# Mean-free output weight and centroids with closed norms in an attention and expert kernel

## The chip, the cores and the metric

One program on one core of a Trainium2 chip. The metric is the device time of one execution in microseconds (us), taken over several executions. The span of a profiled execution is the part of it that the hardware profiler covers. Names of engines: PE is TensorE (PEld its weight loads), DVE is VectorE, ACT is ScalarE, POOL is GpSimd, SP is SyncE, which here only issues DMAs.

## The reference, cut to what matters

The input is 16 batches of 256 tokens of width 128. Attention has 16 heads of width 8 and is causal; behind it come 8 experts with 512 hidden units each, of which each token uses one.

```python
x  = L0_attn_x                                     # 16 x 256 x 128, float32
y  = attention(layernorm(x))                       # V and output weight WO at its end
x2 = x + layernorm(y)
f  = layernorm(x2)
aff    = f @ centroids.T                           # 8 affinities for each token
assign = argmax(aff);  alpha = sigmoid(max(aff))
h  = layernorm(f, ln_g[e], ln_b[e])                # the inner norm, e = assign
z  = alpha * (relu(h @ w1[e].T + b1[e]) @ w2[e].T + b2[e])
out = x2 + layernorm(f + z)
```

## The kernel before

**Stages.** (1) A start: loads, constants, norms of x, and the first projections. (2) The attention loop. (3) A hand-over in which the counts of tokens for each expert become routing tables. (4) The expert stage over 39 tiles of 128 tokens that are sorted by expert. Each engine has a hand-written order; the engines are tied to each other by counted semaphores alone.

**The attention loop** is 20 iterations over 16 batches, software-pipelined. Iteration i works on batch i+3 (`new`: transposes of x and the projections to Q and K), i+1 (`nxt`: scores by query, to find their maxima), i (`t`: scores by key, exponentials, weighing of V), i-1 (`old`: transposes of the output, division), i-2 (`l2`: output projection, norm of y, x2, norm of x2), i-3 (`l3`, `ln`: affinities, choice of the expert) and i-4 (`l4`, `last`: rank within the expert, and the rows to DRAM). PE's iteration has four groups of heads (0 to 3).

- Q and K are split in three bf16 parts: ACT takes the high part from PSUM, DVE forms the residue, ACT the middle part, and POOL the low part (`low`, line 407). SP writes the parts to DRAM (`parts_out`, line 283) and reads them back in the layout of `aug` by six DMAs (`parts_in`, lines 294 and 296). The negated maxima go to `aug` by a DMA too (`shift`, line 306). `scores_near` (line 826) of group 0 waits for that last one.
- `project_qk` (line 773), the transposes and all small products of PE share one PSUM bank, M. Whoever takes it waits until the one before has been copied out (`take_m`).
- The norms of y and x2: DVE takes statistics (line 1115), aggregates (1122) and adds epsilon (`ln_variance`, 1128), POOL raises to the power -1/2 (`power`, 424), DVE applies (`ln_apply`, 1133). This is done three times for each batch: n=0 for y, n=1 for x2, which gives f, and n=2 for f, which is the inner norm. `add_y` (1144) forms x2. PE transposes f (`transpose_f`, 882) and multiplies it with the centroids (894).
- POOL's iteration is: four `select` (the causal mask, lines 413 and 417), with `power` 0 and 1 of batch i-2 between them, then `scatter(last, 0)` (an indirect DMA of 128 rows, line 439), `power(ln, 2)`, `scatter(last, 1)`, `number` (429) and at the end `low` of batch i+3.
- A row in DRAM (`xs_rows`) has 262 floats: f, x2 and six columns.

**The expert stage** is a second software pipeline. At step t: SP loads the weights w1 of a later tile (line 350, a ring of four buffers) and its rows (359, a ring of 14); ACT normalises rows of tile t+3 (702) and, after PE's transpose (976), applies the expert's gain and bias (`enter`, t+2, 721); PE multiplies with w1 (`up`, t+1, 986), ACT and DVE each take two of four relus (731 and 1374), and PE multiplies with w2 (`down_`, t, 999). DVE then handles tile t-1: `add_bias` (1381), `residual` (1389), `statistics` (1394), `aggregate` (1398), `variance` (1403). POOL forms the deviation's inverse (`power_z`, 515) and the bias (`bias_z`, 521), ACT applies both (`apply`, 711), DVE adds x2 (`add_x`, t-3, 1411) and POOL writes the rows of tile t-3 out by an indirect DMA (`leave`, 505). The number of the expert of a tile is only known on the chip: `expert` loads it to a register (`value_load`, which appears as TENSOR_LOAD) on SP, ACT, PE and DVE, since columns and weights are addressed by it.

## Time and profile before

| | us |
|---|---|
| three runs | 473.40, 473.89, 471.58 |
| their median | 473.4 |
| the profiled execution | 472.17 |
| its span | 470.4 |
| outside the span | 1.77 |

| engine | busy us of the span | share |
|---|---|---|
| PE | 364.0 | 77% |
| PEld | 288.5 | 61% |
| DVE | 356.6 | 76% |
| ACT | 255.5 | 54% |
| POOL | 259.7 | 55% |

The mean granted clock of TensorE is 0.928 of full speed. No engine is busy all the time, and the shares are means over stages with different limits. The stages by time: the attention loop in its steady state from about 50 to 290 us, its last iterations to 342, the hand-over to about 363, and the expert stage from there to the end. A row of a timeline has the start, the duration, the engine, line, operation, output<-input, a count if like rows follow each other, and in brackets how long the engine had been idle before it and what released it.

### The profile page before, as it was taken

The page shows a single profiled execution, that of the slowest core. Times are in us where ns is not written, and L with a number is a line of the kernel's source. Part 1 is how long each engine was busy: PE and PEld are TensorE (multiplying, and loading weights), DVE is VectorE, ACT ScalarE, POOL GpSimd, SP SyncE. Part 2 cuts the span into 40 slices and gives each one's busy share as a digit, 9 for nine tenths or more (in the row PEclk, how much of TensorE's full clock was granted, in tenths as well). Part 3 has the DMA queues.
Part 4 walks back from the last instruction along what each step waited for, and adds up shares of the span by engine and source line. Part 5 has one row for each costly group of instructions (what it writes and reads, how often), then busy time and mean ns, then how long its engine had stood idle before and what let it go on. Part 6 is the DMA issues. An engine that isn't in the chain of part 4 may idle for free.

```text
span 470.4 us, 12290 instructions
## 1 busy us (share of the span) xinstructions
PE 364.0 (77%) x3737; PEld 288.5 (61%) x3737; DVE 356.6 (76%) x1281; ACT 255.5 (54%) x574; POOL 259.7 (55%) x388
## 2 busy tenths in 40 slices
PE   3268798798997998798898988986308988888850
PEld 2146566576675776676676766854307877878740
DVE  7658588789989988888878897977532777777770
ACT  2205466566665666567566554672105777776740
POOL 4804425535466467456455565476420677777773
PEclk9999899999999999999989998997556999999995
DMA  7663762563452452552542644021065667676400
GB/s 201 111 102 70 105 113 71 71 106 68 69 108 74 72 108 66 81 103 65 87 92 49 102 98 76 25 71 36 34 194 148 192 199 193 202 196 172 127 26 1
DMA packets 37296, 48.00 MB, mean 102 GB/s; under 512 B 7545, under 2 KB 27133, under 8 KB 35696
## 3 DMA queue, kind: packets, MB, share of 16 engines
q1 hardware_dynamic: 33824, 40.15, 41.4%
q0 software_dynamic: 2832, 6.53, 3.9%
q8 instruction: 31, 0.51, 0.5%
q10 hardware_dynamic: 576, 0.54, 0.3%
q14 instruction: 33, 0.27, 0.3%
HBM read 33.05 MB, written 14.35 MB: 101 GB/s over the span
## 4 chain that ended last, share of the span: by engine, by line
PE 42%; DMA 15%; DVE 14%; issue 11%; POOL 10%; ACT 4%; SPq 2%; DVEq 1%; ACTq 1%; POOLq 0%
DMA aug<-nmT 9%; PE O L847 5%; DMA aug<-qk_parts 4%; PE ST L826 3%; PE S L813 3%; POOL out_x L505 3%; PE M L859 3%; DVE nmf L1074 3%; PE O L851 3%; PE S L986 3%; PE O L999 3%; PE S L808 2%; PE S L806 2%; PE S L803 2%; PE ST L835 2%
## 5 line engine op out<-in xcount | busy, mean ns | idle before, releaser
L1074 DVE TENSOR_REDUCE nmf<-S 128x2 f32<-128x512 f32 (+1 forms) x192 | 130.2, 682 | 41.3 <-PE S L813 20.1
L580 ACT ACTIVATE p<-ST 128x1024 f32<-128x1024 f32 x64 | 65.6, 1025 | 18.8 <-PE ST L826 18.1
L413 POOL TENSOR_SCALAR_AFFINE_SELECT p<-p 128x512 f32<-128x512 f32 x64 | 40.9, 638 | 54.5 <-ACT p L580 54.2
L826 PE MATMUL ST<-aug 128*128 128x256 bf16 x256 | 39.0, 275 | 20.0 <-DMA aug<-nmT 18.5
L813 PE MATMUL S<-aug 126*128 126x128 bf16 x512 | 51.8, 225 | 0.0
L505 POOL DMA_INDIRECT out_x<-vaug,x_all x39 | 41.3, 1060 | 18.6 <-issue 15.4
L1374 DVE TENSOR_SCALAR vaug<-ST,col_tab 128x128 f32<-128x128 f32 x78 | 23.8, 346 | 30.6 <-PE ST L986 13.7
L999 PE MATMUL O<-w_tab,vaug 128*128 x312 | 44.9, 285 | 1.5 <-DVE vaug L1374 1.4
L417 POOL TENSOR_SCALAR_AFFINE_SELECT p<-p 128x512 f32<-128x512 f32 x64 | 41.3, 645 | 7.9 <-ACT p L584 5.5
L813 PEld LDWEIGHTS S<-aug 126*128 126x128 bf16 x512 | 41.3, 101 | 3.8
L847 PE MATMUL O<-p,vaug 128*32 128x256 f32 x512 | 42.3, 401 | 0.9 <-POOL p L413 0.9
L999 PEld LDWEIGHTS O<-w_tab,vaug 128*128 128x128 f32 x312 | 40.2, 195 | 3.0 <-issue 2.4
L424 POOL TENSOR_TENSOR rs_ln<-ve_ln,mhalf 128x2 f32<-128x2 f32 x32 | 22.7, 709 | 33.1 <-DVE ve_ln L1128 32.0
L584 ACT ACTIVATE p<-ST 128x512 f32<-128x512 f32 x64 | 38.7, 605 | 1.4 <-PE ST L835 0.3
L808 PE MATMUL S<-causal,identb 128*128 128x256 bf16 x128 | 36.4, 284 | 3.1 <-DVE nmf L1074 3.0
L826 PEld LDWEIGHTS ST<-aug 128*128 128x128 bf16 x256 | 23.1, 98 | 24.6 <-DMA aug<-nmT 20.5
L439 POOL DMA_INDIRECT xs_rows<-pay,pos x32 | 33.1, 1033 | 8.5 <-issue 6.6
L711 ACT ACTIVATE vaug<-vaug,nbz,rsz 128x128 f32<-128x128 f32 x39 | 19.2, 493 | 31.7 <-POOL nbz L521 31.7
L986 PE MATMUL S<-vaug,w1s 128*128 128x128 f32 x156 | 27.4, 300 | 10.8 <-issue 5.7
L515 POOL TENSOR_TENSOR rsz<-vez,mhalf 128x1 f32<-128x1 f32 x39 | 23.0, 590 | 21.9 <-DVE vez L1403 20.6
L986 PEld LDWEIGHTS S<-vaug,w1s 128*128 128x128 f32 x156 | 21.4, 198 | 18.1 <-issue 17.1
L803 PE MATMUL S<-causal,identb 128*128 128x512 bf16 x64 | 25.4, 396 | 7.3 <-DMA aug<-qk_parts 7.3
(147 smaller groups left out, 900.6 us busy)
## 6 DMA issues: line engine op xcount, KB each, us to landing
w1s<-in_w1t SPq DMA_DIRECT2D x39, 256.0 KB
qk_parts<-qkp SPq DMA_DIRECT2D x16, 384.0 KB, 2.8
aug<-qk_parts SPq DMA_DIRECT2D x32, 192.0 KB
x_all<-xs_rows SPq DMA_DIRECT2D x39, 131.0 KB, 2.6
aug<-qk_parts SPq DMA_DIRECT2D x32, 128.0 KB
aug<-qk_parts SPq DMA_DIRECT2D x32, 64.0 KB
w_tab<-in_w2t SPq DMA_DIRECT2D x8, 256.0 KB, 5.5
out_x<-vaug,x_all POOLq DMA_INDIRECT x39
```

Source lines behind the costliest of these rows:

```text
L413: g.affine_select(out=v, in_=v, compare_op=ALU.is_ge, fill=0.0, base=0, pattern=[[0, 4], [1, P]], channel_multiplier=-1).then_inc(s["sel0" ...
L417: g.affine_select(out=v, in_=v, compare_op=ALU.is_ge, fill=0.0, base=0, pattern=[[0, 4], [1, P]], channel_multiplier=-1).then_inc(s["sel1" ...
L505: g.indirect_dma_start(out=out.rearrange("b t d -> (b t) d"), out_offset=bass.IndirectOffsetOnAxis(ap=xs[:, q, TOK:TOK + 1].bitcast(U32), ...
L580: a.activation(p0[:, gr % 2], ST0[:, :, :], ACT.Exp, scale=SCALE).then_inc(s["exp0"], 1)
L584: a.activation(p1[:, gr % 2], ST1[:, :, :], ACT.Exp, scale=SCALE).then_inc(s["exp1"], 1)
L808: mm(bank.rearrange("p (j c n) -> p j c n", j=2, c=2)[:, :, 1], identb[:, :], causal[:, 0:2], start=True, stop=False)
L813: last = mm(bank[:, j * SEQ + kb * P:j * SEQ + (kb + 1) * P], q[:, h, P:SEQ], k[:, h, kb * P:(kb + 1) * P], start=False, stop=(j == 1 and ...
L826: last = mm(ST0[:, j], kaug[:, p, h, 0:P], qaug[:, p, h], start=True, stop=True)
L847: mm(O[32 * j:32 * j + 32, gr // 2, gr % 2, :], vaug[:, p, 0, 4 * gr + j], p0[:, gr % 2, j], start=True, stop=False)
L986: last = mm(hidden(p, c), w1s[:, t.slot(WR), c * P:(c + 1) * P], nT[:, p], start=True, stop=True)
L999: last = mm(O[:, p, 0, 0:D], hs[:, p, c], w2_tab[:, bass.ds(e * (FC * D) + c * D, D)], start=(c == 0), stop=(c == FC - 1))
L1074: v.tensor_reduce(dst, S[:, n % 2].rearrange("p (j n) -> p j n", j=k), op=ALU.max, axis=AX_X, negate=True).then_inc(s["red"], 1)
```

## The change

The host no longer sends the gains, biases and b1 as tables: they are appended to w1 as six more columns (`w1x`, 518 floats a row), so that a tile's w1 buffer holds them. The output weight has its mean over the width taken out once, on DVE (`centre_wo`), and so have the centroids (`centroid_sums` on PE, `centre_centroids` on DVE). y has no mean then but for rounding, and the affinities can be taken from x2 itself, as a scaled copy of those from f. The norm of f is written in closed form from the variance of x2. Rows in DRAM hold x2 and six columns, 134 floats.

In the expert stage, PE loads the expert's number behind `up`, DVE behind `aggregate`, and ACT no more. SP's weight load also waits for the relus that read the columns. The bias of the last norm moves from POOL to DVE (`z_bias`), `apply`, `add_x` and `leave` come one, one and two steps later, and their small buffers and `zf` have four slots.

```diff
-    TOK, ALPHA, MEAN, VAR, RSTD, SHFT = range(2 * D, 2 * D + 6)
-    ROW = 2 * D + 6
+    TOK, GATE, EPSV, BIAS, RSTD, GAIN = range(D, D + 6)
+    ROW = D + 6
-    UB, XR, OR, WR = 3, 14, 4, 4
+    UB, XR, OR, WR, ZR = 3, 14, 4, 4, 4
-        w1s = sb("w1s", [P, WR, F])
-        col_tab = sb("col_tab", [P, E, 2 + FC])
+        w1s = sb("w1s", [P, WR, FX])
...
-        def column(e, n):
-            return col_tab[:, bass.ds(e, 1), n:n + 1].rearrange("p o n -> p (o n)")
+        def column(t, n):
+            return w1s[:, t.slot(WR), F + n:F + n + 1]
...
             def w1_next(t):
                 e = expert(sp, t)
                 if t.follows(WR):
                     sp.wait_ge(s["h_r"], t.times(2, 2 - 2 * WR))
+                    sp.wait_ge(s["ha_d"], t.times(1, 1 - WR))
+                    sp.wait_ge(s["hd_d"], t.times(1, 1 - WR))
...
             def power(b, n):
-                pool.wait_ge(s["ln_ve"], b.times(3, n + 1))
-                dst = rs_ln[:, n] if n < 2 else pay[:, b.slot(RING), :, RSTD]
-                g.tensor_tensor(dst, ve_ln[:, n], mhalf[:, 0:2], op=ALU.pow).then_inc(s["ln_rs"], 1)
+                pool.wait_ge(s["ln_ve"], b.times(2, n + 1))
+                if n == 0:
+                    ins = g.tensor_tensor(rs_y[:, :], ve_y[:, :], mhalf[:, 0:2], op=ALU.pow)
+                else:
+                    ins = g.tensor_tensor(pay[:, b.slot(RING), :, RSTD:RSTD + 2], ve_x2[:, :, :],
+                                          mhalf[:, 0:4].rearrange("p (t n) -> p t n", n=2), op=ALU.pow)
+                ins.then_inc(s["ln_rs"], 1)
...
                 if t:
                     select(t, 2)
-                if ln:
-                    power(ln, 1)
                 if t:
                     select(t, 3)
                 if last:
                     scatter(last, 0)
                 if ln:
-                    power(ln, 2)
+                    power(ln, 1)
                 if last:
                     scatter(last, 1)
...
-            def bias_z(t):
-                p = t.slot(2)
-                pool.wait_ge(s["rs_z"], t.times(1, 1))
-                g.tensor_scalar(nbz[:, p:p + 1], mvz[:, p, 0:1], rsz[:, p:p + 1], -1.0, ALU.mult, ALU.mult)\
-                    .then_inc(s["nb_z"], 1)
-                    bias_z(n)
-                if n := tile(t, -3):
+                if n := tile(t, -5):
                     leave(n)
...
             def enter(t):
-                e = kept[t.k]
+                act.wait_ge(w1_in[t.slot(WR)], t.turns(WR, 16, 16))
                 act.wait_ge(s["xsT_r"], t.times(1, 1))
-                    kept[n.k] = expert(act, n)
                     enter(n)
...
             def transpose_f(i):
-                pe.wait_ge(s["f_d"], i.times(1, 1))
+                pe.wait_ge(s["x2_d"], i.times(1, 1))
...
             def up(t):
-                kept[t.k] = expert(pe, t)
                     up(n)
+                    kept[n.k] = expert(pe, n)
...
+            def centre_wo(n):
+                if n == 0:
+                    v.bn_stats(st_wo[:, :], wat[:, 3]).then_inc(s["wo_st"], 1)
+                if n == 1:
+                    dve.wait_ge(s["wo_st"], 1)
+                    v.bn_aggr(mv_wo[:, :], st_wo[:, :]).then_inc(s["wo_ag"], 1)
+                if n == 2:
+                    dve.wait_ge(s["wo_ag"], 1)
+                    v.tensor_scalar(wo[:, :], wat[:, 3], mv_wo[:, 0:1], None, ALU.subtract).then_inc(s["wo_d"], 1)
...
             def ln_variance(b, n):
-                dve.wait_ge(s["ln_ag"], b.times(3, n + 1))
-                var = mv_ln[:, n, :, 1] if n < 2 else pay[:, b.slot(RING), :, VAR]
-                v.tensor_scalar_add(ve_ln[:, n], var, EPS).then_inc(s["ln_ve"], 1)
+                dve.wait_ge(s["ln_ag"], b.times(2, n + 1))
+                var = moments(b, n)[:, :, 1]
+                if n == 0:
+                    last = v.tensor_scalar_add(ve_y[:, :], var, EPS)
+                else:
+                    v.tensor_scalar(pay[:, b.slot(RING), :, EPSV], var, EPS, EPS * EPS, ALU.mult, ALU.add)
+                    v.tensor_scalar_add(ve_x2[:, :, 0], var, EPS)
+                    last = v.tensor_scalar(ve_x2[:, :, 1], var, 1.0 + EPS, EPS * EPS, ALU.mult, ALU.add)
+                last.then_inc(s["ln_ve"], 1)
-            def ln_apply(b, n, dst, done):
-                dve.wait_ge(s["ln_rs"], b.times(3, n + 1))
-                for t in (0, 1):
-                    last = v.tensor_scalar(dst(t), ln_src(b, n)(t), mv_ln[:, n, t, 0:1], rs_ln[:, n, t:t + 1],
-                                           ALU.subtract, ALU.mult)
...
             def add_y(b):
-                dve.wait_ge(s["yn_d"], b.times(1, 1))
+                dve.wait_ge(s["ln_rs"], b.times(2, 1))
...
-                v.tensor_tensor(pay[:, p, :, D:2 * D], b.pick(x_all, 2, 2), yn[:, :, :], ALU.add).then_inc(s["x2_d"], 1)
+                for t in (0, 1):
+                    last = v.scalar_tensor_tensor(out=pay[:, p, t, 0:D], in0=yb[:, p, t], scalar=rs_y[:, t:t + 1],
+                                                  in1=b.pick(x_all, 1, 2, t).rearrange("p o d -> p (o d)"),
+                                                  op0=ALU.mult, op1=ALU.add)
...
+            def scale_max(b):
+                dve.wait_ge(s["chosen"], b.times(4, 1))
+                dve.wait_ge(s["ln_rs"], b.times(2, 2))
+                v.tensor_tensor(b.pick(amaxr, 2, 2), b.pick(amax, 2, 2), pay[:, b.slot(RING), :, RSTD],
+                                ALU.mult).then_inc(s["am_d"], 1)
...
             def relu(t):
-                e = kept[t.k]
+                dve.wait_ge(w1_in[t.slot(WR)], t.turns(WR, 16, 16))
...
+            def z_bias(t):
+                z = t.slot(ZR)
+                dve.wait_ge(s["rs_z"], t.times(1, 1))
+                v.scalar_tensor_tensor(out=nbz[:, z:z + 1], in0=mvz[:, z, 0:1], scalar=-1.0, in1=rsz[:, z:z + 1],
+                                       op0=ALU.mult, op1=ALU.mult).then_inc(s["nb_z"], 1)
...
             def tile_step(t):
                 if n := tile(t, -1):
                     add_bias(n)
                     residual(n)
+                if n := tile(t, -3):
+                    z_bias(n)
+                if n := tile(t, -1):
                     statistics(n)
-                if n := tile(t, -3):
+                if n := tile(t, -4):
                     add_x(n)
                 if n := tile(t, 1):
-                    kept[n.k] = expert(dve, n)
                     relu(n)
                 if n := tile(t, -1):
                     aggregate(n)
+                if n := tile(t, 0):
+                    kept[n.k] = expert(dve, n)
+                if n := tile(t, -1):
                     variance(n)
```

What stands on POOL at the end of one attention iteration, before and after. The two indirect DMAs write rows of batch i-4, `pow` is the TENSOR_TENSOR with `mhalf`, `pay,pos` are the rows and their places, and the last row is the low part of Q and K of batch i+3.

```order
L439 DMA xs_rows<-pay,pos 33920x262 [waits al_d,pos_d,id_in,ln_sh]
L424 TENSOR_TENSOR pay<-ve_ln,mhalf 128x2 [waits ln_ve]
L439 DMA xs_rows<-pay,pos 33920x262
L429 COPY pay<-tokid 128x2 [waits x2_d]
L407 TENSOR_TENSOR qkp<-res,qkp 128x512 [waits qk_w0,mid_d]
```

```order
L451 DMA xs_rows<-pay,pos 33920x134 [waits al_d,pos_d,id_in,ln_sh]
L434 TENSOR_TENSOR pay<-ve_x,mhalf 128x2x2 [waits ln_ve]
L451 DMA xs_rows<-pay,pos 33920x134
L441 COPY pay<-tokid 128x2 [waits x2_d]
L415 TENSOR_TENSOR qkp<-res,qkp 128x512 [waits qk_w1,mid_d]
```

The power between the two scatters is now that of the norm of x2, not of f, with four elements for two; the one that stood between two `select` before is gone.

DVE over one tile of the expert stage, before and after. `z_r` and `h_r` are PE's results, `st_z`, `agg_z` and `zf_d` are DVE's own steps, `rs_z` is POOL's power, `zn_d` is ACT's `apply`, and ISA is a register or semaphore instruction.

```order
L1389 SCALAR_TENSOR_TENSOR vaug<-vaug,x_all 128x128 [waits zn_d,zb_d]
L1394 BN_STATS stz<-vaug 128x6 [waits zf_d]
L1411 TENSOR_TENSOR vaug<-vaug,x_all 128x128 [waits out_s1,zn_d]
L255 TENSOR_LOAD eidx
L255 ISA x2
L1374 ISA [waits z_r,h_r]
L1374 TENSOR_SCALAR vaug<-ST,col_tab 128x128
L1374 ISA
L1374 TENSOR_SCALAR vaug<-ST,col_tab 128x128
L1398 BN_AGGR mvz<-stz 128x2 [waits st_z]
L1403 TENSOR_SCALAR vez<-mvz 128x1 [waits agg_z]
```

```order
L1423 SCALAR_TENSOR_TENSOR vaug<-vaug,x_all 128x128 [waits zn_d,zb_d]
L1444 SCALAR_TENSOR_TENSOR nbz<-mvz,rsz 128x1 [waits rs_z]
L1428 BN_STATS stz<-vaug 128x6 [waits zf_d]
L1453 TENSOR_TENSOR vaug<-vaug,x_all 128x128 [waits out_s3,zn_d]
L1408 TENSOR_SCALAR vaug<-ST,w1s 128x128 [waits z_r,h_r,w1_in0]
L1408 TENSOR_SCALAR vaug<-ST,w1s 128x128
L1432 BN_AGGR mvz<-stz 128x2 [waits st_z]
L263 TENSOR_LOAD eidx
L263 ISA x2
L1437 TENSOR_SCALAR vez<-mvz,x_all 128x1 [waits agg_z]
```

The register load moved from in front of the two relus to behind the aggregate, the relus have no register instruction of their own, and one small operation on POOL's result came in ahead of the statistics.

SP over one tile of the expert stage, before and after (the weights, then the rows).

```order
L350 ISA [waits h_r]
L350 DMA w1s<-in_w1t 128x512
L355 TENSOR_LOAD rows_at
L355 ISA x2
```

```order
L358 ISA [waits hd_d,ha_d,h_r]
L358 DMA w1s<-in_w1x 128x518
L363 TENSOR_LOAD rows_at
L363 ISA x2
```

Both register loads stay in SP's queue; the weight load waits for two more semaphores, and carries six more columns.

## Rows read from the trace of the kernel before

**Rows 1.** Windows: stretch, us, busy (count) by engine, granted clock, DMA share, GB/s.

```profile
120.00:200.00 80.00, 70.29 (x842) 54.36 (x835) 70.71 (x247) 49.72 (x106) 45.90 (x66) 1.00 0.44 81
380.00:400.00 20.00, 17.06 (x136) 15.37 (x136) 15.39 (x64) 14.47 (x41) 15.31 (x25) 1.00 0.70 200
```

**Rows 2.** PE's waits over the span (us in total, times, longest); then its timeline.

```profile
PE ST L826 <- DMA aug<-nmT: 18.5, 12, 3.3
...
216.06 0.61 PE L826 MATMUL ST<-aug 128*128 128x256 bf16 x4 [0.63 <-issue]
...
234.96 0.61 PE L826 MATMUL ST<-aug 128*128 128x256 bf16 x4 [1.97 <-DMA aug<-nmT]
```

**Rows 3.** Timelines of PE, POOL and SP in the loop (start, duration).

```profile
106.64 1.13 PE L773 MATMUL M<-xnT,wat 128*128 128x256 f32 x4
...
213.97 1.13 PE L773 MATMUL M<-xnT,wat 128*128 128x256 f32 x4
...
231.52 1.13 PE L773 MATMUL M<-xnT,wat 128*128 128x256 f32 x4
...
268.69 1.13 PE L773 MATMUL M<-xnT,wat 128*128 128x256 f32 x4
...
218.10 0.72 POOL L424 TENSOR_TENSOR pay<-ve_ln,mhalf 128x2 f32<-128x2 f32 x1 [1.98 <-DVE ve_ln L1128]
...
220.22 1.16 POOL L407 TENSOR_TENSOR qkp<-res,qkp 128x512 bf16<-128x512 f32 x1
...
210.85 0.63 SPq L306 DMA_DIRECT2D aug<-nmT  x1
...
228.40 0.63 SPq L306 DMA_DIRECT2D aug<-nmT  x1
```

**Rows 4.** Groups by line and form: count, busy, mean ns, idle before and releaser.

```profile
L424 POOL TENSOR_TENSOR pay<-ve_ln,mhalf 128x2 f32<-128x2 f32 x16 | 11.5, 720 | 27.1 <-DVE ve_ln L1128 27.0
...
L394 POOL TENSOR_TENSOR rsx<-vex,mhalf 128x4 f32<-128x4 f32 x1 | 1.0, 1027 | 2.1 <-DVE vex L1036 2.1
```

**Rows 5.** Timelines of DVE and PE in the last iteration of the loop.

```profile
331.54 0.43 DVE L1144 TENSOR_TENSOR pay<-x_all,yn 128x256 f32<-128x256 f32 x1 [0.45 <-DMA xs_rows<-pay,pos]
...
334.88 0.66 PE L882 MATMUL M<-ident,pay 128*128 128x128 f32 x2 [4.91 <-DVE pay L1133]
```

**Rows 6.** Groups of POOL in the expert stage, by line and form.

```profile
L505 POOL DMA_INDIRECT out_x<-vaug,x_all x39 | 41.3, 1060 | 18.6 <-issue 15.4 <-ACT vaug L711 3.2
L515 POOL TENSOR_TENSOR rsz<-vez,mhalf 128x1 f32<-128x1 f32 x39 | 23.0, 590 | 21.9 <-DVE vez L1403 20.6
...
L521 POOL TENSOR_SCALAR nbz<-mvz,rsz 128x1 f32<-128x1 f32 x39 | 10.3, 264 | 3.8
```

**Rows 7.** Timeline of DVE over one tile of the expert stage.

```profile
400.69 0.61 DVE L1374 TENSOR_SCALAR vaug<-ST,col_tab 128x128 f32<-128x128 f32 x2 [0.45 <-issue]
...
402.46 0.27 DVE L1411 TENSOR_TENSOR vaug<-vaug,x_all 128x128 f32<-128x128 f32 x1
403.19 0.35 DVE L1374 TENSOR_SCALAR vaug<-ST,col_tab 128x128 f32<-128x128 f32 x1 [0.46 <-issue]
```

**Rows 8.** SP's DMA issues at the stage's start and middle; one weight load of PE.

```profile
362.24 0.34 SPq L350 DMA_DIRECT2D w1s<-in_w1t  x1
...
364.80 0.34 SPq L350 DMA_DIRECT2D w1s<-in_w1t  x1
...
367.01 0.34 SPq L350 DMA_DIRECT2D w1s<-in_w1t  x1
...
417.41 0.02 SPq L350 DMA_DIRECT2D w1s<-in_w1t  x1
...
367.65 0.52 PEld L986 LDWEIGHTS S<-vaug,w1s 128*128 128x128 f32 x4 [0.31 <-DMA w1s<-in_w1t]
```

**Rows 9.** Timelines of PE and POOL at the end of the expert stage.

```profile
450.71 0.68 PE L986 MATMUL S<-vaug,w1s 128*128 128x128 f32 x4 [0.19 <-ACT vaug L731]
...
463.25 0.98 POOL L505 DMA_INDIRECT out_x<-vaug,x_all  x1 [0.30 <-issue]
```

More of the change, by code:

```diff
@@ L55, in sandwich_kernel @@
     DH = D // NH
-    E, _, F = w1t.shape
+    E = w1x.shape[0]
+    F = w2t.shape[1] // E
     NT = B * SEQ // P
     FC = F // P
+    FX = F + 2 + FC
+    assert w1x.shape[2] == FX
     NG = NH // 4
@@ L182, in sandwich_kernel @@
         (xs,) = carve(x_all, (XR, ROW))
-        nh, nT, hs, zb, zf, zn, zo = carve(vaug, (2, D), (2, P), (2, FC, P), (2, D), (2, D), (2, D), (OR, D))
+        nh, nT, hs, zb, zf, zn, zo = carve(vaug, (2, D), (2, P), (2, FC, P), (2, D), (ZR, D), (2, D), (OR, D))
         stz = sb("stz", [P, 2, 6])
-        mvz = sb("mvz", [P, 2, 2])
-        vez = sb("vez", [P, 2])
-        rsz = sb("rsz", [P, 2])
-        nbz = sb("nbz", [P, 2])
+        mvz = sb("mvz", [P, ZR, 2])
+        vez = sb("vez", [P, ZR])
+        rsz = sb("rsz", [P, ZR])
+        nbz = sb("nbz", [P, ZR])
         S = ps("S", [P, 2, 512])
@@ L238, in tiles @@
         def tiles(eng, step):
-            for k in range(-3, ST + 3):
+            for k in range(-3, ST + 5):
                 step(Nth(k))
@@ L710, in apply @@
                     act.wait_ge(s["zo_d"], t.times(1, -1))
-                a.activation(zn[:, p], zf[:, p], ACT.Identity, scale=rsz[:, p:p + 1], bias=nbz[:, p:p + 1])\
+                a.activation(zn[:, p], zf[:, z], ACT.Identity, scale=rsz[:, z:z + 1], bias=nbz[:, z:z + 1])\
                     .then_inc(s["zn_d"], 1)
@@ L730, in relu @@
                 for c in range(NA):
-                    last = a.activation(hs[:, p, c], hidden(p, c), ACT.Relu, bias=column(e, 2 + c))
+                    last = a.activation(hs[:, p, c], hidden(p, c), ACT.Relu, bias=column(t, 2 + c))
                 last.then_inc(s["ha_d"], 1)
             act.wait_ge(s["rt"], 1)
-            act.wait_ge(s["w_ffn"], 16 * (E + 3))
-            kept = {}
             def tile_step(t):
@@ L745, in tile_step @@
                     relu(n)
-                if n := tile(t, -2):
+                if n := tile(t, -3):
                     apply(n)
@@ L872, in project_o @@
                 take_m()
+                if i.k == 0:
+                    pe.wait_ge(s["wo_d"], 1)
                 for qb in (0, 1):
-                    last = mm(M[:, qb * P:(qb + 1) * P], onT[:, qb * P:(qb + 1) * P], wat[:, 3], start=True, stop=True)
+                    last = mm(M[:, qb * P:(qb + 1) * P], onT[:, qb * P:(qb + 1) * P], wo[:, :], start=True, stop=True)
                 last.then_inc(s["y_r"], 1)
@@ L884, in transpose_f, with centroid_sums @@
                 m_free[0] = [("fT_d", i.times(1, 1))]
+            def centroid_sums():
+                take_m()
+                pe.wait_ge(s["w_cent"], 16)
+                mm(M[:, 0:E], ones[:, :], cent[:, :], start=True, stop=True).then_inc(s["cm_r"], 1)
+                m_free[0] = [("cm_d", 1)]
             def affinities_and_ranks(n, ln, last):
@@ L932, in step @@
                         transpose_o(old, 0)
+                    if gr == 2 and i.k == 1:
+                        centroid_sums()
                     if gr == 2 and (ln or last):
@@ L1102, in divide, with centre_centroids @@
                                 ALU.mult).then_inc(s["on_d"], 1)
+            def centre_wo(n):
[7 more added lines that the diff above has]
+                    v.tensor_scalar(wo[:, :], wat[:, 3], mv_wo[:, 0:1], None, ALU.subtract).then_inc(s["wo_d"], 1)
+            def centre_centroids():
+                dve.wait_ge(s["cm_r"], 1)
+                v.scalar_tensor_tensor(out=centc[:, :], in0=M[:, 0:E], scalar=-1.0 / D, in1=cent[:, :],
+                                       op0=ALU.mult, op1=ALU.add).then_inc(s["cm_d"], 1)
             def ln_src(b, n):
@@ L1118, in ln_aggregate @@
             def ln_aggregate(b, n):
-                dve.wait_ge(s["ln_st"], b.times(3, n + 1))
+                dve.wait_ge(s["ln_st"], b.times(2, n + 1))
+                if n and b.follows(2):
+                    dve.wait_ge(s["ln_sh"], b.times(1, -1))
                 for t in (0, 1):
-                    dst = mv_ln[:, n, t] if n < 2 else pay[:, b.slot(RING), t, MEAN:MEAN + 2]
-                    last = v.bn_aggr(dst, st_ln[:, n, t])
+                    last = v.bn_aggr(moments(b, n)[:, t], st_ln[:, n, t])
@@ L1147, in choose @@
+                last.then_inc(s["x2_d"], 1)
             def choose(b, n):
@@ L1281, in step @@
                     place(l4, 0)
+                if i.k == 1:
+                    centre_centroids()
                 if l3:
@@ L1314, in step @@
                     count(l3, 0)
-                if l2:
-                    ln_stats(l2, 2)
-                if l3:
                     count(l3, 1)
-                if l2:
-                    ln_aggregate(l2, 2)
-                    ln_variance(l2, 2)
+                if i.k == 0:
+                    for n in range(3):
+                        centre_wo(n)
                 if i.k < 2:
@@ L1373, in relu @@
                 for c in range(NA, FC):
-                    last = v.tensor_scalar(hs[:, p, c], hidden(p, c), column(e, 2 + c), 0.0, ALU.add, ALU.max)
+                    last = v.tensor_scalar(hs[:, p, c], hidden(p, c), column(t, 2 + c), 0.0, ALU.add, ALU.max)
                 last.then_inc(s["hd_d"], 1)
```

110 lines of the change are left out of this document (55 added, 55 removed).

## The prediction, made before the changed kernel ran

> **What bounds the kernel now.** I read the windows first, one in the steady attention loop and one in the expert stage [rows 1]. In the loop PE is busy 70.29 of 80 us and DVE 70.71: two engines near their limit, tied to each other. In the expert stage nobody is: PE 17.06 of 20, DVE 15.39, ACT 14.47, POOL 15.31, so a cycle or a queue sets the pace there.
>
> Next PE's waits [rows 2]. The largest is for the DMA of the negated maxima ahead of `scores_near`: 18.5 us in 12 waits. In one iteration it is 1.97 (234.96); in another (216.06) PE comes last itself. What makes that DMA late stands in [rows 3]: POOL's power 2, the inner norm's, has waited 1.98 for DVE at 218.10, and behind it in POOL's queue are `scatter(last, 1)`, `number` and `low`, which starts at 220.22. SP then writes the parts and reads them back, and the maxima are queued behind these six reads. From `low` to the score they feed it takes 234.96 - 220.22 = 14.74 us. The maxima alone can do it faster: issued at 210.85 they were there by 216.06, after at most 5.21; issued at 228.40 they took until 234.96, 6.56.
>
> `project_qk` marks the iterations: from 106.64 to 268.69 there are nine, 162.05 us, 18.01 each [rows 3]. An undisturbed one is 231.52 - 213.97 = 17.55; it is set by the chain over bank M, which the change leaves as it is.
>
> In the expert stage POOL's queue is the pace, 2.50 us a tile: out_x 1.06, rsz 0.59 and nbz 0.26 busy are 1.91, and 15.4 of "issue" over 39 tiles, 0.39 each, with some small gaps, makes the rest [rows 6]. Its period is DVE's too: 403.19 - 400.69 = 2.50, with 0.46 idle as "issue" in it [rows 7], which is the register load behind `add_x`.
>
> **Start and hand-over: 0.** `centre_wo`, `centroid_sums` and `centre_centroids` are five operations once, on engines that wait in the first iterations. I take no gain from the shorter rows and tables at the start. The bound is 1 us either way.
>
> **Attention loop: -5.** DVE loses two applies for f, two for y that merge with the addition, and a set of statistics, and gains four small operations: as an estimate a tenth of its work, 1.7 of 17.5. That alone is worth nothing where M's chain sets the period; it hides there. POOL loses a power of 0.72, and the one that is left has four elements, 1.03 by the start's power of four [rows 4]. What counts is its place: it is now the power of x2's norm, whose variance is ready several scores before, so the 1.98 of idle goes, less 0.31 for the larger power, and `low` comes some 1.6 earlier. The wait of 1.97 is then nearly covered; next late is M's chain. If every iteration goes at 17.55, nine take 157.95 in place of 162.05: 4.1 less, and with the last one, which has no `project_qk` row in my count, 5. The bound on the small side is 0 (the maxima's landing follows from their own issue), on the large side 8 (M's chain has DVE operations in it, and DVE is freer).
>
> **Last iteration: -2.4.** Transposing f waited 4.91 for DVE's apply and began at 334.88; `add_y` had been done at 331.54 + 0.43 = 331.97 [rows 5]. x2 can now be transposed right then, 2.7 earlier with a hop of 0.2. The ranks need DVE's running counts as well, which I expect to be next late by 0.3. Bounds -1.2 and -3.5. The pads and row reads behind it keep their length.
>
> **Expert stage: -6.3.** Engine by engine, a tile costs:
> - POOL: 1.06 + 0.59 + 0.39 of issue = 2.04, without nbz.
> - DVE: 2.50 less the idle 0.46 is 2.04; `z_bias` adds something between 0 and nbz's 0.26 on POOL. It waits for POOL's power of tile t-3, two tiles old by then; queued behind it are the statistics, `add_x` and the relus. The register load now has relus and the aggregate ahead of it in the queue, against `add_x` alone; I count it hidden, so 2.04 to 2.30.
> - PE: 17.06 of 20 is 2.13 per 2.50 at most, and its register load is behind `up`.
> - SP: its four instructions per tile (two register loads, two DMAs) do not change. Its weight loads of tiles 4 and 28 are at 362.24 and 417.41: 24 tiles in 55.17, 2.30 each [rows 8]. That is faster than the tiles leave, so it is SP's own pace, and it becomes the bound. I add 0.05 for two more semaphores and take **2.35**. The waits are for the relus of tile t-4; behind them are the rows of a tile, which are far ahead in their ring of 14, so only the weights matter.
>
> The weights of tile 38 then leave at 362.24 + 34 x 2.35 = 442.1. One issued at 364.80 was used at 367.65, 2.85 later [rows 8]: so 445.0. ACT's `enter` now waits for them too, since the gain and bias are in that buffer; it and its hop stand between, some 1.2 as an estimate from two relus of 0.61 [rows 7] and two hops. `up` of tile 38 starts near 446.2, against 450.71 [rows 9]: 4.5 less. From there to the last output DMA it was 463.25 - 450.71 = 12.5 with a DVE that had fallen behind; I take 10.8, between 12.5 (unchanged) and 9 (nothing else queued in the last steps). That is 1.7 more. Bounds of this stage: -3 and -9.
>
> The profiled run is 472.17 with 1.77 outside its span of 470.4. Sum: -5 - 2.4 - 6.3 = -13.7, a span of 456.7 and a run of **458.5**. The median of the runs is 473.4, 1.2 above the profiled one; I don't add that.
>
> **A rule weighed.** The register load and issue pair of SP costs 1.10 here: two pairs make the 367.01 - 364.80 = 2.21 of a tile without a stall [rows 8], and with stalls the mean is 2.30. The Trainium skill ("DMA: Bandwidth & Descriptors", "Latency and other measured facts") gives a floor of about 600 ns for a `tensor_load`. By it a pair with its issue of 0.34 would be 0.94, SP 1.9 a tile, and DVE would decide. The rows show more, and they decide.
>
> **The rivals.**
> 1. *The loop gives nothing* (the maxima land by their own issue at 228.40, which ACT's copy sets and not `low`). For it: 6.56 after that issue. Against: only 5.21 after the one at 210.85, so the queue ahead of them matters. 472.17 - 2.4 - 6.3 = 463.5.
> 2. *The expert stage keeps 2.50*: SP's pace is really made by its landing transfers or by ring waits, as its later loads suggest, which keep step with the tiles. The stage then gives only the end: 1.7. 472.17 - 5 - 2.4 - 1.7 = 463.1.
> 3. *More*: SP holds 2.20 (34 x 0.15 = 5.1 less, were DVE as fast), or M's chain shortens by DVE's relief. 450 to 454.
> 4. *Slower: the register load on DVE lies bare.* Behind it is `variance`, on which POOL's power, ACT's apply and `add_x` hang. From `add_x`'s start at 402.46 to the relu at 403.19 is 0.73 [rows 7]: the whole load. With it and 0.26 for `z_bias` a tile costs 2.04 + 0.73 + 0.26 = 3.03, so 37 tiles take 0.53 x 37 = 19.6 more; with the 7.4 of the other stages the run is 472.17 + 19.6 - 7.4 = 484.4. It decides over POOL's 2.50 from 0.46 bare, and makes the whole slower from 2.70 a tile. Against it: even behind a single 0.27 operation only 0.46 of the load shows. The Trainium skill ("Advanced Engine Details and Errata", "Engine Queue Depths") gives VectorE a queue of 8, by which the load would run ahead while relus and aggregate are still queued; the trace agrees so far that part of the load (0.27 of 0.73) is covered.
> 5. *It doesn't do what it says*: the gains in each stage go into other waits, as M's chain and SP's stalls both take what is freed. About 471 to 473.
>
> **How the numbers follow.** Forecast (455 to 462) 0.53; rival 1 0.12; rival 2 0.12; rival 3 0.12; rival 4 0.06; rival 5 0.05. A measurement here can tell about 0.5%, 2.4 us, from no change. Forecast and rivals 1 to 3 are faster: 0.89. Rival 5 is the same, 0.05; rival 4 slower, 0.06. For 8 in 10 the range takes in the forecast, rivals 1 and 2 with some room, and the near end of rival 3: 452 to 465.5.
>
> **What would show it.** In the loop: POOL's power between the two scatters without idle, `low` 4.7 after the start of `project_qk`, where it was 220.22 - 213.97 = 6.25, waits for the maxima well below 18.5 in all, and periods of 17.55. At the loop's end: the transposes of x2 within 0.3 of `add_y`. In the expert stage: tiles 2.35 apart, SP's queue without waits, PE waiting for w1 through ACT's enter, POOL and DVE with idle time that others release. The prediction is wrong if the period of the loop stays near 18.0, if DVE shows idle "issue" ahead of `variance`, or if output DMAs stay 2.50 apart.

## The result and the profile after

The changed kernel takes **453.9 us** (median of four runs, 452.74 to 456.57), against 473.6 of before on the same chip: a ratio of 0.959, 95% interval 0.954 to 0.965. The forecast was 458.5, with a range of 452 to 465.5. The profiled run is 454.81 with a span of 453.1, 17.3 below before's 470.4; the sum had said 13.7.

The page of the changed kernel, engines' busy time in the span:

```profile
span 453.1 us, 11940 instructions
PE 359.6 (79%) x3739; PEld 286.3 (63%) x3739; DVE 336.5 (74%) x1244; ACT 250.8 (55%) x574; POOL 242.1 (53%) x334
```

Windows of the changed kernel, the answers to [rows 1] (stretch, us, busy by engine, granted clock, DMA share, GB/s):

```profile
120.00:200.00 80.00, 73.49 (x885) 57.31 (x883) 64.89 (x229) 52.22 (x111) 46.10 (x63) 1.00 0.47 78
385.00:405.00 20.00, 18.91 (x146) 16.89 (x147) 17.93 (x77) 15.01 (x44) 14.14 (x19) 1.00 0.65 175
```

In the loop DVE has 64.89 of 80 us where it had 70.71, and PE 73.49 where it had 70.29: PE now goes faster through the same work. In the expert stage PE (18.91 of 20) and DVE (17.93) are much fuller, POOL emptier. The expert window of before and this one are both at the full granted clock (1.00).

The loop, the answer to [rows 3]: PE and POOL timelines of the changed kernel.

```profile
109.11 1.13 PE L772 MATMUL M<-xnT,wat 128*128 128x256 f32 x4
...
230.32 1.13 PE L772 MATMUL M<-xnT,wat 128*128 128x256 f32 x4
247.56 1.13 PE L772 MATMUL M<-xnT,wat 128*128 128x256 f32 x4
264.80 1.13 PE L772 MATMUL M<-xnT,wat 128*128 128x256 f32 x4
...
231.43 1.04 POOL L451 DMA_INDIRECT xs_rows<-pay,pos  x1 [0.19 <-issue]
232.50 1.05 POOL L434 TENSOR_TENSOR pay<-ve_x,mhalf 128x4 f32<-128x4 f32 x1
233.75 1.04 POOL L451 DMA_INDIRECT xs_rows<-pay,pos  x1 [0.19 <-issue]
234.79 0.20 POOL L441 COPY pay<-tokid 128x2 int32<-128x2 int32 x1
234.94 1.18 POOL L415 TENSOR_TENSOR qkp<-res,qkp 128x512 bf16<-128x512 f32 x1
```

The power between the scatters no longer waits, `low` starts 4.6 us after `project_qk` (234.94 - 230.32; 6.25 before), and nine iterations take 264.80 - 109.11 = 155.7 us, 17.30 each, where they took 162.05. The last ones are 17.24 apart.

PE still waits for the maxima's DMA (14.7 us over the span, 18.5 before), but these waits no longer hold the loop up. Followed back from the end, the chain of the kernel before runs through that DMA in the disturbed iterations, as in these two of its rows (start, duration, what):

```profile
192.15 7.05 DMA aug<-nmT
228.40 6.50 DMA aug<-nmT
```

The chain of the changed kernel has no such piece from 178 us to the last of these `project_qk`.

The end of the loop, the answer to [rows 5]: DVE and PE timelines, then PE's of before for the running counts.

```profile
325.21 0.61 DVE L1172 SCALAR_TENSOR_TENSOR pay<-yb,rs_y,x_all 128x128 f32<-128x128 f32 x2 [3.66 <-DMA xs_rows<-pay,pos]
325.97 0.66 PE L883 MATMUL M<-ident,pay 128*128 128x128 f32 x2 [2.26 <-DVE pay L1172]
...
331.90 0.58 PE L905 MATMUL M<-hot,before 128*128 128x16 f32 x2 [2.27 <-DVE run L1203]
```

```profile
339.92 0.58 PE L899 MATMUL M<-hot,before 128*128 128x16 f32 x2 [1.96 <-DVE run L1172]
```

The expert stage, the answer to [rows 7 to 9]: SP's issues, one tile of DVE, and the last `up` and output DMA.

```profile
402.67 0.35 SPq L358 DMA_DIRECT2D w1s<-in_w1x  x1
403.77 0.35 SPq L367 DMA_DIRECT2D x_all<-xs_rows  x1
404.93 0.34 SPq L358 DMA_DIRECT2D w1s<-in_w1x  x1
406.03 0.34 SPq L367 DMA_DIRECT2D x_all<-xs_rows  x1
...
403.02 0.17 DVE L1432 BATCH_NORM_AGGREGATE mvz<-stz 128x2 f32<-128x6 f32 x1
403.22 0.21 DVE L1437 TENSOR_SCALAR vez<-mvz,x_all 128x1 f32<-128x1 f32 x1
404.71 0.29 DVE L1453 TENSOR_TENSOR vaug<-vaug,x_all 128x128 f32<-128x128 f32 x1
405.11 0.61 DVE L1408 TENSOR_SCALAR vaug<-ST,w1s 128x128 f32<-128x128 f32 x2
...
407.43 0.61 DVE L1408 TENSOR_SCALAR vaug<-ST,w1s 128x128 f32<-128x128 f32 x2
...
434.70 0.61 PE L993 MATMUL S<-vaug,w1s 128*128 128x128 f32 x4
...
445.91 0.97 POOL L516 DMA_INDIRECT out_x<-vaug,x_all  x1 [0.30 <-issue]
```

The register load on DVE stands between the first two of these DVE rows, and no idle time shows there. The two longest waits between 370 and 420 us (who, for what, us in total, times, longest); SP itself has no wait in that stretch:

```profile
ACT vaug L724 <- DMA w1s<-in_w1x: 12.7, 21, 1.2
POOL rsz L526 <- DVE vez L1437: 11.3, 21, 1.1
```

Where the span went, from the two traces (a pad is a DMA that fills the rows behind an expert's last token; the first is taken at its register load):

| stretch | before | after | forecast | measured |
|---|---|---|---|---|
| to the last issue of the maxima | 307.66 | 302.64 | -5 | -5.0 |
| from there to the first pad | 34.4 | 31.4 | -2.4 | -3.0 |
| to SP's fifth w1 load | 20.2 | 19.2 | 0 | -1.0 |
| to `up` of the last tile | 88.5 | 81.5 | -4.5 | -7.0 |
| to the last output DMA | 12.5 | 11.2 | -1.7 | -1.3 |

### The profile page after: what moved, and what is told of

Same layout as the page of the kernel before. It is cut to its first block, busy times and chain, and to the rows that moved or that the text cites. A ratio compares the mean times of both kernels' runs of the same rounds, so it can differ in the third digit from the quotient of the medians.

```text
span 453.1 us, 11940 instructions
## 1 busy us (share of the span) xinstructions
PE 359.6 (79%) x3739; PEld 286.3 (63%) x3739; DVE 336.5 (74%) x1244; ACT 250.8 (55%) x574; POOL 242.1 (53%) x334
## 4 chain that ended last, share of the span: by engine, by line
PE 54%; DMA 11%; DVE 9%; issue 9%; POOL 6%; SPq 5%; ACT 4%; POOLq 0%; DVEq 0%; ACTq 0%
PE O L846 6%; DMA aug<-nmT 6%; PE O L1006 5%; PE ST L825 5%; PE S L812 4%; PE S L993 4%; PE M L858 3%; PE M L772 3%; PE S L807 3%; PE S L805 3%; PE S L802 3%; PE O L850 3%; PE ST L993 2%; PE ST L834 2%; POOL out_x L516 2%
## 5 line engine op out<-in xcount | busy, mean ns | idle before, releaser
L583 ACT ACTIVATE p<-ST 128x1024 f32<-128x1024 f32 x64 | 65.5, 1023 | 16.6 <-PE ST L825 15.9
L825 PE MATMUL ST<-aug 128*128 128x256 bf16 x256 | 39.9, 279 | 14.9 <-DMA aug<-nmT 14.7
L812 PEld LDWEIGHTS S<-aug 126*128 126x128 bf16 x512 | 41.2, 101 | 3.8
L1006 PE MATMUL O<-w_tab,vaug 128*128 x312 | 42.6, 280 | 0.0
L846 PE MATMUL O<-p,vaug 128*32 128x256 f32 x512 | 41.2, 391 | 0.3 <-POOL p L421 0.3
L1006 PEld LDWEIGHTS O<-w_tab,vaug 128*128 128x128 f32 x312 | 37.8, 191 | 1.0 <-issue 0.2
L825 PEld LDWEIGHTS ST<-aug 128*128 128x128 bf16 x256 | 23.4, 99 | 19.5 <-DMA aug<-nmT 17.1
L1408 DVE TENSOR_SCALAR vaug<-ST,w1s 128x128 f32<-128x128 f32 x78 | 23.7, 345 | 14.8 <-PE ST L993 12.8
L415 POOL TENSOR_TENSOR qkp<-res,qkp 128x512 bf16<-128x512 f32 x16 | 18.7, 1168 | 20.3 <-ACT qkp L559 20.3
L805 PEld LDWEIGHTS S<-aug 126*128 126x128 bf16 x256 | 21.1, 103 | 9.7 <-issue 2.2
```

What stands on the lines that cost most here:

```text
L583: a.activation(p0[:, gr % 2], ST0[:, :, :], ACT.Exp, scale=SCALE).then_inc(s["exp0"], 1)
L812: last = mm(bank[:, j * SEQ + kb * P:j * SEQ + (kb + 1) * P], q[:, h, P:SEQ], k[:, h, kb * P:(kb + 1) * P], start=False, stop=(j == 1 and ...
L825: last = mm(ST0[:, j], kaug[:, p, h, 0:P], qaug[:, p, h], start=True, stop=True)
L846: mm(O[32 * j:32 * j + 32, gr // 2, gr % 2, :], vaug[:, p, 0, 4 * gr + j], p0[:, gr % 2, j], start=True, stop=False)
L1006: last = mm(O[:, p, 0, 0:D], hs[:, p, c], w2_tab[:, bass.ds(e * (FC * D) + c * D, D)], start=(c == 0), stop=(c == FC - 1))
```

## The experiments

Each kernel was timed in rounds with the kernel before on the same chip. Medians of the same kernel differ between chips by some 4 us, and the traces say where: the seventh `project_qk` comes between 104.7 and 110.1 us in kernels whose start is nearly the same work. Part of that is TensorE's clock. In every trace PE has waited 1.8 to 3.4 us for the maxima at about 90 us. The mean granted clock from 90 to 100 us is then 1.00 in the two traces with the earliest seventh `project_qk` (`b_low_first`, 104.67; `a_dve_fill`, 105.06), 0.66 in the one with the latest (`a_sp4_nocheck_w6`, 110.14) and 0.83 in all others, before and the changed kernel among them. So runs are compared with others on the same chip, or by their ratio to before, and lengths of stages are read from each trace. "Per tile" is the spacing of the output DMAs over 25 tiles: 2.53 before (2.50 undisturbed). In the changed kernel it is 2.31. Three more traces have the same expert stage, and their scatter is the scale for small differences: 2.34 (`a_again`), 2.37 (`a_dve_fill`), 2.38 (`a_low_late`).

**The changed kernel again** (`a_again`), as the scale for the next three, which ran beside it.

> The changed kernel once more, beside the others of this call. It sets the scale for them: 453.9 us as before, iterations of the attention loop 17.24 us apart from the seventh on, project_qk to low 4.62 us, output DMAs 2.3 us apart.

457.9 us, ratio 0.966 (0.962 to 0.971). 17.33 us an iteration; the seventh `project_qk` at 108.2.

**Low ahead of the power, in the kernel before** (`b_low_first`).

```diff
-                if ln:
-                    power(ln, 2)
                 if last:
                     scatter(last, 1)
...
                     low(b)
+                if ln:
+                    power(ln, 2)
```

> The kernel before with one edit: POOL's power 2 (the inner norm's) stands behind low, not ahead of the second scatter. Theory A (low's place gives the loop's gain): low comes 4.6 us after project_qk in place of 6.25, the waits for the maxima shrink, the iterations go to 17.24 to 17.55 us, and the run is 3.5 to 5.5 us shorter, 468 to 470. Theory B (DVE's relief gives it): low is earlier but the iterations keep their mean of 18.0, and the run stays at 472 to 474.

464.2 us, ratio 0.981 (0.976 to 0.985): 8.8 us less than before on the same chip, with one instruction moved. Two `project_qk` of its trace, nine iterations apart:

```profile
104.67 1.13 PE L773 MATMUL M<-xnT,wat 128*128 128x256 f32 x4
...
260.28 0.92 PE L773 MATMUL M<-xnT,wat 128*128 128x256 f32 x3
```

155.6 us, 17.29 each, as in the changed kernel, with all of DVE's old work in place, and the chain of these iterations has no DMA of the maxima. Theory A stands, and the gain is larger than forecast. Of the 8.8, 6.4 lie in these nine iterations. The two traces differ by another 2.0 at the seventh `project_qk` (104.67 against 106.64), which is within the scatter of the start.

**DVE's work put back** (`a_dve_fill`): two `tensor_scalar` or `bn_stats` of 128x128 on scratch at each of three places.

```diff
+                if l2:
+                    filler(l2, 0)
...
+                if l2:
+                    filler(l2, 2)
...
+                if l2:
+                    filler(l2, 4)
```

> The changed kernel with DVE work put back for nothing: in each iteration four tensor_scalar of 128x128 and two bn_stats of 128x128 on scratch, at the places where the applies and the third statistics stood (some 2.3 us). Theory A: these hide, the iterations stay at 17.24 and the run within 1 us of the changed kernel. Theory B: the iterations go back to 17.6 to 18.0 us, and the run is 4 to 6 us longer, 458 to 460.

454.7 us, against 457.9 of `a_again` beside it; iterations of 17.36. DVE is as busy as in the kernel before (160.1 of the 180 us from 110 to 290, 158.7 before, 145.8 in the changed kernel). The 3 us are the scatter of the start (seventh `project_qk` at 105.1, against 108.2). DVE's relief in the loop is worth nothing that shows.

**Low late** (`a_low_late`).

```diff
                 if b := at(i, 3):
+                    if ln:
+                        for n in range(2):
+                            g.tensor_tensor(pad_p[:, n], ones[:, 0:2], mhalf[:, 0:2], op=ALU.pow)
                     low(b)
```

> The changed kernel with two small powers of no use on POOL (some 0.72 us each) ahead of low. Theory A: low comes 6.1 us after project_qk, scores_near waits more for the maxima, the iterations go to 17.6 to 18.0, and the run is 3 to 5 us longer, 457 to 459. Theory B: low is late and nothing follows from it, the run stays within 1 us.

462.6 us, 4.7 more than `a_again`; `low` comes 6.0 us after `project_qk` and iterations are 17.92. POOL and PE in its trace:

```profile
254.31 1.40 POOL L511 TENSOR_TENSOR pad_p<-ones,mhalf 128x2 f32<-128x2 f32 x2
255.69 1.15 POOL L416 TENSOR_TENSOR qkp<-res,qkp 128x512 bf16<-128x512 f32 x1
...
252.71 0.61 PE L829 MATMUL ST<-aug 128*128 128x256 bf16 x4 [1.54 <-DMA aug<-nmT]
```

1.4 us on one queue cost 0.6 an iteration, and the DMA of the maxima is back in the chain. With the other two this settles the loop.

**Four registers with one load on SP** (`a_sp4`).

```diff
-                e = expert(sp, t)
+                e = many(eidx, t.k, E - 1)
...
+                    _, vals = nc.values_load_multi_w_load_instructions(
+                        table[0:1, n:n + k], engines=[sp.engine], min_val=0, max_val=top)
```

> The changed kernel in which SP loads the numbers of four tiles with one register load (24 of them over the stage in place of 78), so that a tile costs SP two issues of 0.35 us and half a load. Theory S (SP's queue is the bound of the expert stage, 2.25 us a tile without stalls): the weights come early, ACT's enter no longer waits for them (12.7 us in 21 waits over 50 us before), and the stage goes to PE's and DVE's 2.05 to 2.15 us a tile, 5 to 8 us less, a run of 446 to 449. Theory T (the transfers or the ring of four set the pace): the issues move earlier or wait for the ring, but tiles stay 2.25 to 2.35 apart, and the run within 2 us of 453.9.

447.6 us, ratio 0.948 (0.940 to 0.956), 2.21 per tile, below all four traces with the changed kernel's expert stage. SP's queue was the bound, but not much behind it comes something else: ACT still waits 12.1 us in 50 for w1, now in few long pieces. The trace shows two gaps between issues for each four tiles, in which SP loads four numbers and checks them:

```profile
399.64 0.33 SPq L380 DMA_DIRECT2D x_all<-xs_rows  x1
401.90 0.34 SPq L371 DMA_DIRECT2D w1s<-in_w1x  x1
404.21 0.33 SPq L380 DMA_DIRECT2D x_all<-xs_rows  x1
```

**DVE's register load back ahead of the relus** (`a_load_front`).

```diff
                 if n := tile(t, 1):
+                    kept[n.k] = expert(dve, n)
                     relu(n)
...
-                if n := tile(t, 0):
-                    kept[n.k] = expert(dve, n)
```

> The changed kernel with DVE's register load back in front of the relus, where it was before. Theory S: DVE has 0.2 us a tile to spare under SP's 2.3, and the load shows as 0.45 of idle, so DVE becomes the bound at 2.4 to 2.5 a tile and the run is 4 to 8 us longer, 458 to 462. Rival: it is hidden by the waits that DVE has anyway, and the run stays within 1 us.

460.0 us, ratio 0.970 (0.962 to 0.977), 2.45 per tile. The ratio alone doesn't tell it from the changed kernel's 0.959 and 0.966; the pace lies above all four, and the load is bare again as in [rows 7]:

```profile
401.58 0.61 DVE L1408 TENSOR_SCALAR vaug<-ST,w1s 128x128 f32<-128x128 f32 x2 [0.28 <-issue]
```

**The bias back on POOL** (`a_zbias_pool`).

```diff
                     power_z(n)
+                    bias_z(n)
...
-                if n := tile(t, -3):
-                    z_bias(n)
```

> The changed kernel with the bias of the last norm back on POOL behind its power. POOL then costs 1.04 + 0.57 + 0.26 + issue 0.4 = 2.3 a tile, about SP's pace: tiles 2.3 to 2.5 apart, the run 0 to 6 us longer. If POOL was the bound before because of this one operation, the output DMAs go back to 2.50 us apart and the run to 460; if SP binds, the run stays at 454 to 455.

462.5 us, ratio 0.978 (0.971 to 0.985), 2.50 per tile: the pace of before. POOL's timeline is full again:

```profile
402.33 0.57 POOL L526 TENSOR_TENSOR rsz<-vez,mhalf 128x1 f32<-128x1 f32 x1
403.00 0.37 POOL L532 TENSOR_SCALAR nbz<-mvz,rsz 128x1 f32<-128x1 f32 x1
403.72 1.06 POOL L516 DMA_INDIRECT out_x<-vaug,x_all  x1 [0.35 <-issue]
```

**Wide rows** (`a_wide`).

```diff
-    ROW = D + 6
+    ROW = 2 * D + 6
```

> The changed kernel with rows of 262 floats in DRAM (the columns behind the sixth are zeros that nobody reads, set once on DVE), in place of 134. If the shorter rows gave the 0.7 us between the last pad and the first row read, and nothing in the expert stage, the run is 1 us longer, 455. If DMA traffic was part of the pace of the expert stage (share 0.70 before, 0.64 after), tiles go to 2.4 us apart, and the run is 3 to 5 us longer.

457.1 us, ratio 0.966 (0.959 to 0.974), 2.38 per tile. The time is within the scatter of the changed kernel itself (0.959 and 0.966), and so is the pace: `a_low_late`, with narrow rows, has 2.38 too. In the expert stage the width of the rows costs nothing that shows. The hand-over is another matter. SP's issues of its four pads and of the first row reads, in this kernel and then in the changed one:

```profile
332.75 4.32 SPq L274 DMA_DIRECT2D xs_rows<-fill  x4
341.21 3.63 SPq L367 DMA_DIRECT2D x_all<-xs_rows  x4
```

```profile
335.01 3.66 SPq L274 DMA_DIRECT2D xs_rows<-fill  x4
342.17 3.63 SPq L367 DMA_DIRECT2D x_all<-xs_rows  x4
```

From the first pad to the first row read it is 8.5 us with wide rows and 7.2 with narrow ones. The two other traces with wide rows that were read for it (before, `b_low_first`) have 8.2 and 9.0, and the six others with narrow rows and one register load for each number have 7.3 to 7.6. So the shorter rows do gain about 1 us there.

**The stages of before** (`a_early_bias`).

```diff
-                if n := tile(t, -3):
+                if n := tile(t, -2):
                     z_bias(n)
...
-                if n := tile(t, -4):
+                if n := tile(t, -3):
                     add_x(n)
...
-                if n := tile(t, -5):
+                if n := tile(t, -3):
                     leave(n)
...
-                if n := tile(t, -3):
+                if n := tile(t, -2):
                     apply(n)
```

> The changed kernel with the stages of before: z_bias and ACT's apply at tile t-2, add_x and leave at t-3 (the bias is still on DVE). Theory L (the later stages are part of the gain, since DVE otherwise waits for POOL's power one tile after its variance): z_bias waits some 0.2 us in each tile, tiles go from 2.3 to 2.5 us apart or more, and the run is 5 to 9 us longer, 459 to 463. Rival (taking the bias off POOL was enough, and the stages only add steps at the end): the pace stays at 2.3 and the run is 1 to 3 us shorter.

479.9 us, ratio 1.011 (1.003 to 1.018): **about 1% slower than before**, 3.04 per tile. Three engines wait for each other in a ring:

```profile
402.67 1.03 POOL L516 DMA_INDIRECT out_x<-vaug,x_all  x1 [1.40 <-ACT vaug L714]
403.73 0.58 POOL L526 TENSOR_TENSOR rsz<-vez,mhalf 128x1 f32<-128x1 f32 x1
...
404.34 0.16 DVE L1444 SCALAR_TENSOR_TENSOR nbz<-mvz,rsz 128x1 f32<-128x1 f32 x1 [1.00 <-POOL rsz L526]
```

POOL's power stands behind an output DMA of 1.03, DVE's bias waits 1.00 for it, and the next output DMA waits 1.40 for what follows from the bias. Between 370 and 420 us, some 16 tiles, POOL, ACT and DVE each wait 17 times for the one before in the ring (24.0, 21.8 and 16.6 us). The direction is Theory L's, the size (22 to 26 us over the two medians of the changed kernel) some three times its. All these stages were moved at once, so which of them closes the ring isn't told apart.

**Four-fold loads on SP, PE and DVE, six w1 buffers** (`a_multi_w6`), and the same with `low` ahead of the power (`a_multi_low_w6`).

```diff
-    UB, XR, OR, WR, ZR = 3, 14, 4, 4, 4
+    UB, XR, OR, WR, ZR = 3, 14, 4, 6, 4
```

> The changed kernel with one register load for four tiles on SP, DVE and PE alike, and six w1 buffers in place of four. In the kernel with four-fold loads on SP alone (tiles 2.17 us apart) ACT still waited 12.1 us in 50 for w1. If the ring of four buffers is what then makes w1 late, these waits go, the stage runs at PE's and DVE's 2.0 to 2.1 us a tile, and the run is 3 to 5 us below that kernel, 443 to 446. If the landing of transfers sets the pace, or PE does, it stays at 2.17 and 447.

> The same, and POOL's power 1 behind low, not ahead of the second scatter, so that low comes 3.6 us after project_qk in place of 4.62. The period of 17.24 us is then that of PE's own chain over bank M and should not move; what may go are the waits of the first iterations and the scatter of their lengths: 0 to 2 us less than the kernel above. More than 3 us less would mean that the maxima still bind.

453.9 and 453.1 us, ratios 0.956 and 0.955 (0.949 to 0.964 and 0.946 to 0.964): not faster than `a_sp4`. The first has 2.30 per tile. On DVE the loads of four numbers, which were hidden one by one, come in one piece that no queue hides:

```profile
402.79 0.29 DVE L1437 TENSOR_TENSOR vaug<-O,b_tab 128x128 f32<-128x128 f32 x1 [1.35 <-issue]
```

In the same place the first four matmuls of `up` take 1.06, not 0.68, and the granted clock of that 10 us is 0.83. In the second, `low` comes 3.6 us after `project_qk` in place of 4.6, and most iterations stay at 17.24: an earlier `low` gains nothing more.

**Four-fold loads on SP alone, no range check behind them, six buffers** (`a_sp4_nocheck_w6`).

```diff
                         table[0:1, n:n + k], engines=[sp.engine], min_val=0, max_val=top,
+                        skip_runtime_bounds_check_because="the tables are clamped to this range")
```

> The changed kernel with one register load for four tiles on SP alone (PE and DVE load each tile's number as in the changed kernel), without the range check that follows each loaded value on SP (0.15 + 0.02 us and gaps, about 0.24 us a value; the tables are clamped when they are made), and six w1 buffers. SP then costs 8 x 0.53 + 2 x 0.3 = 4.8 us for four tiles, 1.2 a tile. With four-fold loads and the checks, a burst of 1.5 us stood in SP's queue twice in four tiles and ACT waited 12.1 us in 50 for w1. If SP's queue was all that kept the stage from the pace of PE and DVE, tiles go to 2.0 to 2.1 us apart and the run is 2 to 5 us below that kernel, 443 to 446. If w1's transfer takes over or PE's own instructions and its register load set 2.15, it stays at 447.

**445.4 us**, ratio 0.933 (0.925 to 0.941), 2.02 per tile, the fastest of all, though its seventh `project_qk` came latest (110.1). The window:

```profile
380.00:400.00 20.00, 18.64 (x162) 18.18 (x161) 18.60 (x88) 16.37 (x49) 16.39 (x20) 1.00 0.69 190
```

PE (18.64 of 20) and DVE (18.60) are nearly full, and the stage is at their pace. The check and the ring were taken away together, so their shares are not told apart.

## Why the prediction was right, and where it was off

**The time.** 453.9 is 4.6 below the forecast. It lies in the range, but just below the 455 to 462 that the forecast itself took in, and inside the 450 to 454 of rival 3. Neither mechanism of rival 3 came: SP did not hold 2.20, and DVE's relief did not shorten the loop. So the path was right and several terms were too small. That `a_again` came out at 457.9, close to the forecast, is the scatter of the start.

**Bounds.** That a queue paces the expert stage of the kernel before, and that it is POOL's, was right: `a_zbias_pool` gives back 2.50 by one operation of 0.26 alone.

**Loop.** The mechanism was right; the period was mis-sized. The forecast took 17.55 for undisturbed, since five of nine iterations of before had it, and named M's chain as its cause. Undisturbed is 17.24, in the changed kernel and in `b_low_first`, so the 17.55 iterations were held by the late `low` as well; the first of the nine in the kernel before (106.64 to 123.88) already had 17.24. Nine iterations gave 6.4, not 4.1. Some 0.9 of that is one iteration of before, 19.62 long where the other late ones have 18.70, in which the granted clock was at the lower level from about 236 to 239 us, behind PE's wait of 1.97 at 234.96. The iterations behind the nine gave another 1.1. This profile's start was 2.5 us later (109.11 against 106.64), which is scatter. That the stage came out at exactly the forecast 5.0 is luck, the sum of these three. Rival 1 (the maxima land by their own issue) falls with `a_low_late` and `b_low_first`.

**DVE's relief** was costed at nothing, and is nothing (`a_dve_fill`).

**End of the loop.** 3.0, forecast 2.4, and the match is partly luck. The transposes did move right behind `add_y`, as forecast. The running counts were then late by more than the 0.3 that the forecast allowed: they begin 6.1 us behind the end of `add_y` (331.90 - 325.82), where they began 8.0 behind it before (339.92 - 331.97). So this step gave 1.9 in place of 2.4. The other 1.1 lies ahead of `add_y`, in a stretch that the forecast left as it was. What `add_y` waits for there is the rows of an earlier batch to have left `pay`: 3.66 us, where DVE had been idle 0.45 for them before [rows 5]. What made that stretch shorter was not tried.

**Hand-over.** Forecast 0, with 1 us either way; 1.0 came. It is the shorter rows, which the forecast had put at nothing: with wide rows in the same kernel (`a_wide`) the way from the first pad to the first row read is 1.3 longer, and to the fifth w1 load 19.5 in place of 18.2.

**Expert stage.** SP as the next bound, at 2.35 a tile, was right: 24 loads in 409.42 - 353.21 = 56.2, 2.34 each, with no wait of SP's queue, and `a_sp4` shows it by experiment. The mean hides two kinds: most of these loads are 2.25 apart, 0.05 more than before as forecast, and five are 2.6 to 2.7, with no wait that would say why. Mis-sized was the end of the stage. The forecast let the last weight loads go at 2.35 too, but SP has read its last rows by then, and the last three go 1.15 to 1.7 behind one another. The last load leaves 76.4 us behind the fifth, where 79.9 was forecast, and the stage to the last `up` gained 7.0 in place of 4.5. Rival 2 falls.

**The rule weighed.** The chain of the changed kernel has SP's register loads and issues ahead of the expert stage (start, duration, what):

```profile
341.45 0.27 SPq L363
342.17 0.34 SPq L367
342.55 0.27 SPq L363
```

The load's row is 0.27 long and the issue's 0.34, and a pair comes every 1.10; in between stand the register arithmetic and the range check. The Trainium skill ("DMA: Bandwidth & Descriptors", "Latency and other measured facts") has about 600 ns as the load's floor. The load's row is below that here, and the pair with all that belongs to it is above the 0.94 that the prediction estimated from the page's figure. The pair is what the kernel pays.

**Rival 4** did not come. In its place, behind the aggregate, DVE's load shows no idle time (403.02 and 403.22). Where it is bare, ahead of the relus (`a_load_front`), a tile costs 2.45, not 3.03, since only some 0.3 of it shows (4.6 us in 16 waits between 370 and 420 us). The Trainium skill ("Advanced Engine Details and Errata", "Engine Queue Depths") gives VectorE a queue of eight entries. The trace agrees as far as one load goes, which was covered behind relus and aggregate; four in one piece were not (1.35 idle). The way to a slower kernel was another, and no rival had it: the bias on DVE without the later stages, 1.011 of before.

## What to carry to other kernels

An operation's place in a queue can cost more than its work: one power of 0.72 us, with its wait, ahead of an operation that a DMA chain hangs on was worth 8.8 us in the run (6.4 of them within nine iterations of the trace, and some 2 more that may be scatter), where the whole change was worth 15.1 on the same chip. Undoing that needed none of the algebra. When an operation moves to another engine, look at the stages of its producer and consumers too: left as they were here, three engines waited for each other in a ring. Count the queue that only issues DMAs as an engine too: register loads and their checks are its work, and several values can come with one load where nothing urgent stands behind it.

## What the runs showed of the hardware that was not expected

- One register load of four values and its checks holds SP's queue for about 1.9 us between two issues (399.64 to 401.90, less the issue's 0.33). With one value it is 0.75 (402.67 to 403.77, less 0.35), so four at once cost 0.5 each.
- In `a_multi_w6` PE's mean granted clock was 0.83 over 400 to 410 us, inside a busy stage. Windows of 1 us have PE busy 0.08, 0.77 and 0.37 us in the three from 398 to 401, and the granted clock at 0.50, the lower of its two levels, from 402 to 404. The changed kernel has 1.00 there.

```profile
400.00:410.00 10.00, 9.37 (x70) 9.19 (x69) 6.89 (x33) 7.52 (x23) 5.70 (x8) 0.83 0.65 185
```

- The early part varies by some 5 us between traces (seventh `project_qk` 104.7 to 110.1), and everything behind it moves along. All have the wait for the maxima at about 90 us, and they differ in whether the granted clock falls behind it. That does not account for all: traces with the same 0.83 there still lie between 106.0 and 109.5. What decides it was not tried.
